# Scan stage of a two-layer block: another order of ScalarE's evictions, and the last step without its state update

## The chip, the cores and the metric

The kernel runs on one NeuronCore of a Trainium2 chip, as one program written engine by engine, with semaphores set by hand. The metric is the device time of one execution in microseconds (us). PE is TensorE, ACT ScalarE, DVE VectorE, POOL GpSimd, and SP issues the DMA transfers.

## The reference

Two layers are computed. Only the first is touched here. Its attention is a scan over mini-batches of 16 tokens (32 steps for 4 sequences of 512 tokens, 32 heads of 16), which carries a state W1, b1:

```python
def step(carry, x):
    W1_s, b1_s = carry
    xq, xk, xv, eta_mb = x
    Z1 = xk @ W1_s + b1_s
    grad = _ln_fused_l2_bwd(Z1, xv - xk, ln_w, ln_b)
    Attn1 = jnp.tril(xq @ xk.swapaxes(-1, -2))
    b1_bar = b1_s - jnp.tril(eta_mb) @ grad
    Z1_bar = xq @ W1_s - eta_mb * Attn1 @ grad + b1_bar
    W1_new = W1_s - (last_eta * xk).swapaxes(-1, -2) @ grad
    b1_new = b1_s - jnp.sum(last_eta * grad, axis=-2, keepdims=True)
    out = xq + _ln(Z1_bar, ln_w, ln_b)
    return ((W1_new, b1_new), out)
_, ys = jax.lax.scan(step, init, xs)      # the state behind the last step is dropped
```

Beside it runs the first layer's feed-forward part, which does not depend on the scan:

```python
g = jnp.einsum('th,ih->ti', xf, gate_w) * gate_s
u = jnp.einsum('th,ih->ti', xf, up_w) * up_s
hdn = jax.nn.silu(g) * u
out = jnp.einsum('ti,hi->th', hdn, down_w) * down_s
```

The second layer (latent attention and a mixture of experts) follows and makes up the larger part of the time.

## The kernel before

The stage in question is one block, from about 196 to 858 us of the span. It interleaves two kinds of work in a written order, `for n in range(END)` on every engine, END = 44. Each engine takes its own list strictly in order.

**The scan.** Steps n = 0 to 31 (`NSTEP` = 32) each carry the state once round the engines. PE computes the step's product into `zbank` (`z_product`, L833 and L836). ACT squares it (L1035), DVE reduces, ACT takes the root (L1037), and then DVE runs a chain of twelve small instructions (L1130 to L1148) that ends in the scaled gradient `sg`. DVE and ACT copy two blocks each of it into `sg_bd` (L1154, L1058). PE's `state_update` (L849) needs all four copies. DVE adds the result to `w_state` (L1088), DVE and ACT spread it into `w_x` (L1094, L949), and the next `z_product` reads that. POOL sums the gradients for the bias (`sum_s`, L721 and L723).

**The outputs of the scan** come `LAG` = 9 steps later, in groups G of four parts. `scores` (L877) needs `q_bd` from ACT (L967), DVE masks the result into `pt` (L1114), `outputs` (L903) adds to `obank`. A group is closed by ACT (`o_sb`, `o_sq`), `variances` on PE (L911), a root on ACT (`o_std`, L1043), four reciprocals on DVE (L1167), a product on POOL (L792), the scale and bias on ACT (L1024, the first thing in `late`), and an addition to `q_t` on POOL (L798). From n = 32 to 43 this work and the rest of the feed-forward part stand alone; call it the tail.

**The feed-forward part** is a list of jobs, `gate`, `up` and `down`, each a group of matmuls (L60 to L62) into one of two PSUM banks by turns, so that a job can start only when the one two places before it is evicted. The list runs gate, up, gate, up; before each third's four `down` jobs the next third's first gate has been put. A step of the scan is cut in four pieces (`ffn(n, 0)` to `ffn(n, 3)`), and a job's ACT and POOL work is done in the piece in which its last matmul falls. ACT evicts a gate with Silu (`silu_g`, L1003) and an up with a copy (L1009). POOL multiplies the two (`product`, L741). ACT rounds the product to its high half `hid_hi` (`high`, L991; in two halves at L988 near a `down`), and POOL subtracts for the low half (`low`, L747). ACT does the high half of up j-1 just ahead of the eviction of gate j.

Silu and the root are in different tables of ACT, so a load of 1.28 us (ACT_TABLE_LOAD, under L1003 or L1033) stands ahead of the first Silu behind a root.

Of the kernel before, what the change touches and what calls it, by code (L numbers as in the profile page):

```python
# [69 lines left out]
def build(nc, A, out):  # L70
    with ExitStack() as outer:
# [486 lines left out]
        with ExitStack() as st:  # L558
# [82 lines left out]
            with nc.Block() as block:  # L641
# [63 lines left out]
                def _(pool):  # L705
# [71 lines left out]
                    for n in range(END):  # L777
                        ffn(n, 0)
                        if n < NSTEP:
                            sum_s(n)  # L780
# [22 lines left out]
                def _(pe):  # L803
# [110 lines left out]
                    for n in range(END):  # L914
# [10 lines left out]
                        if n < NSTEP:  # L925
                            state_update(n)
                            if n + 1 < NSTEP:
                                turn_k(n + 1)
# [13 lines left out]
                def _(act):  # L942
# [50 lines left out]
                    def ffn(n, i):  # L993
                        for j in ended(n, i):
                            t, kind, a, o = JOBS[j]
                            x, bank = nth(j), fb[j % 2]
                            if j >= 1 and kind_of(j - 1) == "up" and kind != "down":
                                high(j - 1)
# [13 lines left out]
                            else:  # L1012
                                if x >= 2:
# [3 lines left out]
                                                     scale=small[:, SM["down_s"] + o:SM["down_s"] + o + 1]).then_inc(ev_down, 1)  # L1017

                    def late(n):
                        G = finish_at(n)  # L1020
                        if G is not None:
                            g = G % NF
                            act.wait_ge(oxh_done, G + 1)
                            nc.scalar.activation(o_y[:], o_y[:], ACT.Identity, scale=small[:, SM["ttt_w"] + g:SM["ttt_w"] + g + 1],  # L1024
                                                 bias=small[:, SM["ttt_b"] + g:SM["ttt_b"] + g + 1]).then_inc(oy_done, 1)
                        ffn(n, 3)

                    expand(0)
                    turned_k(0)
                    for n in range(END):  # L1030
# [21 lines left out]
                        if n < NSTEP:  # L1052
                            act.wait_ge(sg_done, n + 1)
                            if n == 0:
                                act.wait_ge(zero_done, 2)
                            for b in (2, 3):
                                r = slice(32 * b, 32 * b + 32)
                                nc.scalar.activation(sg_bd[r, b, :], sg[r, n % 2, :], ACT.Copy).then_inc(sgbd_act, 1)  # L1058
# [20 lines left out]
                def _(dve):  # L1079
# [44 lines left out]
                    for n in range(END):  # L1124
                        ps = parts_at(n)
                        if n < NSTEP:
# [22 lines left out]
                            dve.wait_ge(sg_done, n + 1)  # L1149
                            if n == 0:  # L1150
                                dve.wait_ge(zero_done, 2)
                            for b in (0, 1):
                                r = slice(32 * b, 32 * b + 32)
                                nc.vector.tensor_copy(sg_bd[r, b, :], sg[r, n % 2, :]).then_inc(sgbd_dve, 1)  # L1154
# [1098 lines left out]
```

## Time and profile before

| | us |
|---|---|
| median of three runs | 2019.95 (2014.51 to 2021.71) |
| the profiled execution | 2020.42 |
| its span (first to last instruction) | 2018.8 |

Busy time of the engines over the span, from the profile's page:

| engine | busy us | share |
|---|---|---|
| PE | 1879.5 | 93% |
| DVE | 1228.3 | 61% |
| POOL | 1023.7 | 51% |
| ACT | 983.4 | 49% |

PE is the busy engine in the whole program, but a mean over unlike stages says little about one of them. The stage is read by asking, for each pause of PE, which wait ended last. The releaser that a row names is the last by the profile; where a row says "issue", the profile shows none, and the instruction on the other engine that ended just before the pause has to be looked up by its time.

### The profile page before, as it was taken

To read this page: it belongs to the slowest core of one execution; us is meant where nothing else is said; L and a number is where in the kernel's file an instruction comes from. 1 tells how busy PE (TensorE), PEld (TensorE's weight loads), DVE (VectorE), ACT (ScalarE), POOL (GpSimd) and SP (SyncE) were. 2 spreads that over 40 slices of the span, in tenths; PEclk is the share of its full clock that TensorE was granted. 3 is DMA by queue.
4 is the path that set the end of the run, shared out by engine and by line. 5 is a ranking of instruction groups with operands and counts; after the bars stand their busy time and mean duration, and the time that the engine had idled before them with its cause. 6 is when DMAs were issued, how large, how long until landed. Compare 5 with 4: busy or idle time off the path is not lost. (4 is left out here: it accounts for less than half of the span.)

```text
span 2018.8 us, 34603 instructions
## 1 busy us (share of the span) xinstructions
PE 1879.5 (93%) x12536; PEld 1416.2 (70%) x12536; DVE 1228.3 (61%) x2417; ACT 983.4 (49%) x2117; POOL 1023.7 (51%) x896
## 2 busy tenths in 40 slices
PE   5898899998999999799899989999999999999998
PEld 3676777666666665487777866777777777777776
DVE  4663566688788864367345446666666666666663
ACT  3332556556565655445434335444444444444442
POOL 5444566566565644520143337555555555555552
PEclk9998999999999999989999999999999999999999
DMA  7885657336334533132678861232333223322320
GB/s 239 281 302 184 224 168 265 117 116 219 107 115 146 190 100 107 61 128 85 231 241 284 264 229 43 95 115 95 105 115 115 95 88 132 113 75 76 106 101 33
DMA packets 157111, 297.96 MB, mean 148 GB/s; under 512 B 20240, under 2 KB 97296, under 8 KB 150288
## 3 DMA queue, kind: packets, MB, share of 16 engines
q1 hardware_dynamic: 155856, 294.70, 43.3%
q8 instruction: 102, 1.67, 0.3%
q10 hardware_dynamic: 1088, 1.05, 0.2%
q14 instruction: 65, 0.53, 0.1%
HBM read 221.52 MB, written 74.19 MB: 146 GB/s over the span
## 5 line engine op out<-in xcount | busy, mean ns | idle before, releaser
L1996 POOL TENSOR_SCALAR probs<-probs,rsum 128x512 f32<-128x512 f32 x256 | 396.6, 1567 | 247.5 <-DVE rsum L2132 247.5
L2096 ACT ACTIVATE p_tok<-bank 128x512 fp32r<-128x512 f32 x256 | 154.9, 608 | 345.7 <-PE bank L2036 345.6
L2128 DVE TENSOR_REDUCE nmax<-bank 128x1 f32<-128x512 f32 x256 | 158.9, 683 | 93.7 <-PE bank L2028 93.7
L2138 DVE TENSOR_TENSOR p_tok<-bank,p_tok 128x512 fp32r<-128x512 f32 x256 | 173.4, 680 | 16.2 <-ACT p_tok L2096 16.2
L2088 ACT ACTIVATE probs<-bank,nmax 128x512 f32<-128x512 f32 x256 | 173.0, 693 | 2.2 <-DVE nmax L2128 2.2
L60 PE MATMUL bank<-xs,ffn_w 128*128 128x512 f32 x352 | 154.9, 440 | 12.7 <-issue 9.2
L1484 POOL TENSOR_TENSOR y_pieces<-y_tok,y_pieces 128x512 fp32r<-128x512 f32 x48 | 64.2, 1351 | 188.4 <-ACT y_pieces L1689 188.4
L2036 PE MATMUL bank<-ident,probs 128*128 128x128 f32 x1024 | 156.5, 277 | 2.8 <-DVE p_tok L2138 2.8
L2036 PEld LDWEIGHTS bank<-ident,probs 128*128 128x128 f32 x1024 | 122.4, 141 | 51.0 <-issue 27.4
L61 PE MATMUL bank<-xs,ffn_w 128*128 128x512 f32 x352 | 140.4, 399 | 0.0
L62 PE MATMUL bank<-xs,ffn_w 128*128 128x512 f32 x352 | 140.1, 398 | 0.0
L1114 DVE SCALAR_TENSOR_TENSOR pt<-bank,t_mask 128x256 f32<-128x256 f32 x256 | 91.8, 414 | 77.5 <-PE bank L877 76.0
L741 POOL TENSOR_TENSOR hid<-up_down_sb,silu_g 128x256 f32<-128x256 f32 x88 | 66.6, 777 | 101.7 <-issue 76.7
L759 POOL TENSOR_TENSOR ff_acc<-ff_acc,up_down_sb 128x256 f32<-128x256 f32 x96 | 73.5, 790 | 81.0 <-ACT up_down_sb L1016 81.0
L60 PE MATMUL bank<-p_tok,ckv_tok 128*128 128x512 f32 x256 | 106.2, 415 | 5.5 <-DVE qk L1303 2.9
L2024 PE MATMUL bank<-qk 64*128 64x512 f32 x768 | 106.9, 410 | 3.1 <-PEq L1381 3.1
L2144 DVE TENSOR_TENSOR ctx<-bank,ctx 128x512 fp32r<-128x512 f32 x64 | 44.3, 692 | 102.1 <-ACT ctx L2104 102.1
L60 PEld LDWEIGHTS bank<-xs,ffn_w 128*128 128x128 f32 x352 | 67.6, 192 | 50.8 <-issue 35.4
L60 PE MATMUL bank<-ctx,uvo 128*128 128x512 f32 x240 | 99.9, 416 | 2.3 <-issue 2.3
L62 PE MATMUL bank<-p_tok,ckv_tok 128*128 128x512 f32 x256 | 100.6, 393 | 0.0
L61 PE MATMUL bank<-p_tok,ckv_tok 128*128 128x512 f32 x256 | 100.1, 391 | 0.0
L62 PE MATMUL bank<-ctx,uvo 128*128 128x512 f32 x240 | 94.9, 395 | 0.0
(281 smaller groups left out, 4930.8 us busy)
## 6 DMA issues: line engine op xcount, KB each, us to landing
ffn_w<-ffn_pieces SPq DMA_DIRECT2D x120, 512.0 KB, 3.7
uvo<-uvo_pieces SPq DMA_DIRECT2D x15, 2048.0 KB, 7.8
wq<-wq_pieces SPq DMA_DIRECT2D x16, 1536.0 KB, 6.4
ffn_pieces<-stage SPq DMA_DIRECT2D x30, 512.0 KB, 4.2
xs<-xn_pieces SPq DMA_DIRECT2D x4, 2048.0 KB, 8.0
y_tok<-in_gup SPq DMA_DIRECT2D x32, 256.0 KB, 3.7
wk<-wk_pieces SPq DMA_DIRECT2D x16, 512.0 KB, 3.7
ffn_w<-ffn_pieces SPq DMA_DIRECT2D x16, 384.0 KB, 3.5
```

The costliest lines, as they stand in the source:

```text
L60: nc.tensor.matmul(o, w_hi, x_hi, start=start, stop=False)
L61: nc.tensor.matmul(o, w_hi, x_lo, start=False, stop=False)
L62: return nc.tensor.matmul(o, w_lo, x_hi, start=False, stop=stop)
L759: ins = nc.gpsimd.tensor_tensor(acc[:, o, h], acc[:, o, h], dn_sb[:, d % 2, h], ALU.add)
L1114: nc.vector.scalar_tensor_tensor(out=pt[:, p % 2, i, :, :], in0=psp[i][:, 0:2 * SUPER].rearrange("p (h t) -> p h t", h=2), scalar=1.0, in1 ...
L1996: nc.gpsimd.tensor_scalar(probs[:, u % 8, :], probs[:, u % 8, :], rsum[:, u % 8:u % 8 + 1], None, ALU.mult).then_inc(norm_done, 1)
L2024: nc.tensor.matmul(banks[hh][:], ten[r, a, 0, tile, q], ten[r, b, 1, tile, :], start=(a + b == 0), stop=False)
L2036: ins = nc.tensor.transpose(banks[4 + u % 2][:, kt * P:(kt + 1) * P], probs[:, u % 8, kt * P:(kt + 1) * P], ident[:])
L2088: nc.scalar.activation(probs[:, u % 8, :], banks[u % HG][:], ACT.Exp, bias=nmax[:, u % 8:u % 8 + 1], scale=1.0, accum_out=rsum[:, u % 8:u ...
L2096: nc.scalar.activation(p_tok[:, Q % 2, 0, :, hh * P:(hh + 1) * P], banks[4 + u % 2][:].rearrange("p (k q) -> p k q", k=NBLK), ACT.Copy).th ...
L2128: nc.vector.tensor_reduce(nmax[:, u % 8:u % 8 + 1], banks[u % HG][:], axis=X_AXIS, op=ALU.max, negate=True).then_inc(max_done, 1)
L2138: nc.vector.tensor_tensor(p_tok[:, Q % 2, 1, :, q], banks[4 + u % 2][:].rearrange("p (k q) -> p k q", k=NBLK), p_tok[:, Q % 2, 0, :, q].bi ...
```

## The change

Three things are changed, all in the scan stage.

1. In ACT's `ffn`, where a gate follows an up and is not itself followed by a `down`, the gate is evicted first and the up's high half is taken behind it. This holds for 32 gates. A gate right ahead of a `down` keeps the old order.
2. The scale of a group's outputs (L1024 before) is taken out of the head of `late`: for n < 32 it now stands behind `ffn(n, 3)`, for n >= 32 still ahead of it.
3. At the last step of the scan PE's `state_update`, the four copies into `sg_bd` and POOL's `sum_s` are left out.

```diff
@@ gpsimd
-                        if n < NSTEP:
+                        if n + 1 < NSTEP:
                             sum_s(n)
@@ tensor
-                        if n < NSTEP:
+                        if n + 1 < NSTEP:
                             state_update(n)
-                            if n + 1 < NSTEP:
-                                turn_k(n + 1)
+                            turn_k(n + 1)
@@ scalar
-                            if j >= 1 and kind_of(j - 1) == "up" and kind != "down":
+                            after_up = j >= 1 and kind_of(j - 1) == "up" and kind != "down"
+                            if after_up and kind_of(j + 1) == "down":
                                 high(j - 1)
                             act.wait_ge(f_ready, j + 1)
...
+                            if after_up and kind_of(j + 1) != "down":
+                                high(j - 1)
+
+                    def scale_output(n):
...
+                    def late(n):
+                        if n >= NSTEP:
+                            scale_output(n)
                         ffn(n, 3)
+                        if n < NSTEP:
+                            scale_output(n)
...
-                        if n < NSTEP:
+                        if n + 1 < NSTEP:
                             act.wait_ge(sg_done, n + 1)
@@ vector
-                            dve.wait_ge(sg_done, n + 1)
...
-                                nc.vector.tensor_copy(sg_bd[r, b, :], sg[r, n % 2, :]).then_inc(sgbd_dve, 1)
+                            if n + 1 < NSTEP:
+                                dve.wait_ge(sg_done, n + 1)
...
+                                    nc.vector.tensor_copy(sg_bd[r, b, :], sg[r, n % 2, :]).then_inc(sgbd_dve, 1)
```

ACT's list at the start of step 15 before, from the root of the step (`st_s`) to its copies of the gradient (`o_std` is a group's outputs, `hid_hi` the high half, `silu_g` an evicted gate, `up_down_sb` an evicted up):

```order
L1037 ACTIVATE st_s<-st_v,eps 128x16
L1024 ACTIVATE o_std<-o_std,small 128x512
L991 ACTIVATE hid_hi<-hid 128x512
L1003 ACT_TABLE_LOAD
L1003 ACTIVATE silu_g<-bank,ffn_scales 128x512
L967 ACTIVATE q_bd<-q_t,cols 128x128 x2
L1009 ACTIVATE up_down_sb<-bank,ffn_scales 128x512
L991 ACTIVATE hid_hi<-hid 128x512
L1003 ACTIVATE silu_g<-bank,ffn_scales 128x512
L967 ACTIVATE q_bd<-q_t,cols 128x128 x2
L977 ACTIVATE grad_bd<-grad_j 128x4x16 x2
L1058 ACTIVATE sg_bd<-sg 32x256 x2
```

The same place in the changed kernel:

```order
L1045 ACTIVATE st_s<-st_v,eps 128x16
L1003 ACT_TABLE_LOAD
L1003 ACTIVATE silu_g<-bank,ffn_scales 128x512
L990 ACTIVATE hid_hi<-hid 128x512
L1026 ACTIVATE o_std<-o_std,small 128x512
L966 ACTIVATE q_bd<-q_t,cols 128x128 x2
L1009 ACTIVATE up_down_sb<-bank,ffn_scales 128x512
L1003 ACTIVATE silu_g<-bank,ffn_scales 128x512
L990 ACTIVATE hid_hi<-hid 128x512
L966 ACTIVATE q_bd<-q_t,cols 128x128 x2
L976 ACTIVATE grad_bd<-grad_j 128x4x16 x2
L1066 ACTIVATE sg_bd<-sg 32x256 x2
```

The table load and the gate's eviction have come forward past the scale of the outputs and the high half; the number of table loads in the whole list is the same, 62. The scale of outputs passes a feed-forward eviction in five steps (14, 18, 22, 26 and 30); in 14 and 18 that eviction is a gate's with a table load.

PE's list at the last step of the scan, with the rows that are gone marked:

```order
 L61 MATMUL bank7<-xs,ffn_w 128x512
 L62 MATMUL bank7<-xs,ffn_w 128x512
-L849 MATMUL bank0<-sg_bd,ktz 32x64 x16
 L903 MATMUL bank1<-pt,grad_bd 32x128 x8
 L60 MATMUL bank7<-xs,ffn_w 128x512
```

Behind the feed-forward matmuls PE now goes straight to a group's outputs, which need nothing of this step's gradient.

## Rows read from the trace of the kernel before

**Rows 1.** Windows: the 32 scan steps; us, busy time (x instructions), clock, DMA share, GB/s.

```profile
196.00:741.00 545.00, 501.37 (x4758) 356.53 (x4759) 406.06 (x838) 324.90 (x686) 328.19 (x389) 0.98 0.50 165
```

**Rows 2.** Waits of PE, 196 to 742 us: total us, times, longest us.

```profile
PE bank L60 <- issue: 14.5, 12, 2.1
PE bank L849 <- DVE sg_bd L1154: 13.9, 15, 1.9
```

**Rows 3.** Timeline of ACT, step 15: start us, us, instruction, [idle before <-releaser].

```profile
453.90 0.80 ACT L1024 ACTIVATE o_std<-o_std,small 128x512 f32<-128x512 f32 x1
454.60 0.62 ACT L991 ACTIVATE hid_hi<-hid 128x512 fp32r<-128x512 f32 x1
455.24 1.28 ACT L1003 ACT_TABLE_LOAD   x1
456.53 0.69 ACT L1003 ACTIVATE silu_g<-bank,ffn_scales 128x512 f32<-128x512 f32 x1
...
463.52 0.85 ACT L1058 ACTIVATE sg_bd<-sg 32x256 f32<-32x256 f32 x2
```

**Rows 4.** Timeline of PE, step 15: next gate's first matmul, state update.

```profile
457.32 0.58 PE L60 MATMUL bank<-xs,ffn_w 128*128 128x512 f32 x1 [2.05 <-issue]
...
464.47 0.65 PE L849 MATMUL bank<-sg_bd,ktz 128*32 128x64 f32 x32 [0.35 <-issue]
```

**Rows 5.** Timeline of ACT and of PE, step 4.

```profile
272.54 0.63 ACT L991 ACTIVATE hid_hi<-hid 128x512 fp32r<-128x512 f32 x1 [1.87 <-POOL hid L741]
...
275.27 0.47 PE L60 MATMUL bank<-xs,ffn_w 128*128 128x512 f32 x1 [0.76 <-issue]
...
279.55 0.65 PE L849 MATMUL bank<-sg_bd,ktz 128*32 128x64 f32 x32
```

**Rows 6.** Timeline of DVE, ACT and PE, step 12: copies of the gradient, state update.

```profile
409.92 0.77 DVE L1154 COPY sg_bd<-sg 32x256 f32<-32x256 f32 x2
410.55 0.85 ACT L1058 ACTIVATE sg_bd<-sg 32x256 f32<-32x256 f32 x2
411.50 0.65 PE L849 MATMUL bank<-sg_bd,ktz 128*32 128x64 f32 x32 [1.27 <-DVE sg_bd L1154]
```

**Rows 7.** Timeline of ACT and PE, step 25.

```profile
638.67 0.85 ACT L1058 ACTIVATE sg_bd<-sg 32x256 f32<-32x256 f32 x2 [1.46 <-DVE sg L1148]
...
639.65 0.65 PE L849 MATMUL bank<-sg_bd,ktz 128*32 128x64 f32 x32
```

**Rows 8.** Timeline of ACT and PE, step 31 and the first matmul of step 32.

```profile
744.71 0.85 ACT L1058 ACTIVATE sg_bd<-sg 32x256 f32<-32x256 f32 x2
745.66 1.08 PE L849 MATMUL bank<-sg_bd,ktz 128*32 128x64 f32 x32 [3.88 <-issue]
...
754.18 1.13 PE L911 MATMUL bank<-o_sq,avg 128*128 128x512 f32 x2
```

**Rows 9.** Line L1144 (DVE, two SBUF inputs): ns least/median/most, first and last start us.

```profile
L1144 DVE TENSOR_TENSOR t<-t x32: 424/638/930, 209.0 to 741.1; 128x256 f32<-128x256 f32 x32
```

**Rows 10.** Timeline of POOL, ACT and PE, steps 32 and 33.

```profile
758.09 1.43 POOL L747 TENSOR_TENSOR hid_lo<-hid,hid_hi 128x256 fp32r<-128x256 f32 x2 [4.13 <-ACT hid_hi L991]
759.47 1.29 POOL L730 TENSOR_TENSOR w_snap_x<-w_snap,bd 128x512 f32<-128x512 f32 x1
762.24 1.29 POOL L792 TENSOR_TENSOR o_std<-o_sb,o_std 128x512 f32<-128x512 f32 x1 [1.48 <-DVE o_std L1167]
763.56 0.81 ACT L1024 ACTIVATE o_std<-o_std,small 128x512 f32<-128x512 f32 x1 [3.26 <-POOL o_std L792]
765.01 0.71 PE L877 MATMUL bank<-q_bd,k_t 32*128 32x256 f32 x8 [0.88 <-ACT q_bd L967]
```

**Rows 11.** Windows behind and in long pauses of PE: columns as in rows 1.

```profile
457.60:460.90 3.30, 3.30 (x9) 2.52 (x8) 3.06 (x8) 1.41 (x3) 1.62 (x2) 0.50 0.18 66
...
600.30:602.20 1.90, 0.00 (x0) 0.00 (x0) 1.76 (x5) 1.89 (x3) 0.81 (x2) 1.00 0.25 101
602.30:605.70 3.40, 3.40 (x41) 2.14 (x45) 2.34 (x6) 1.81 (x7) 1.75 (x2) 1.00 0.24 73
```

More of the change, by code:

```diff
@@ L1017, in ffn @@
                                                      scale=small[:, SM["down_s"] + o:SM["down_s"] + o + 1]).then_inc(ev_down, 1)
-                    def late(n):
+                            if after_up and kind_of(j + 1) != "down":
+                                high(j - 1)
+                    def scale_output(n):
                         G = finish_at(n)
@@ L1148, in _ @@
                             nc.vector.tensor_tensor(hd(sg[:, n % 2, :]), hd(t1[:]), over_d(st_f[:]), ALU.mult).then_inc(sg_done, 1)
-                            dve.wait_ge(sg_done, n + 1)
[L1150 to L1153, printed above, removed]
-                                nc.vector.tensor_copy(sg_bd[r, b, :], sg[r, n % 2, :]).then_inc(sgbd_dve, 1)
+                            if n + 1 < NSTEP:
+                                dve.wait_ge(sg_done, n + 1)
+                                if n == 0:
+                                    dve.wait_ge(zero_done, 2)
+                                for b in (0, 1):
+                                    r = slice(32 * b, 32 * b + 32)
+                                    nc.vector.tensor_copy(sg_bd[r, b, :], sg[r, n % 2, :]).then_inc(sgbd_dve, 1)
                         if ps:
```

## The prediction

> **What bounds the kernel now.** I read the windows first. In the 545 us of the 32 scan steps PE is busy for 501, at a mean clock of 0.98 [rows 1]: 44 us are pauses, and only they can be won by another order. Next PE's waits, to see what the pauses are. Two kinds lead: 14.5 us in 12 pauses ahead of a feed-forward job (L60, "issue"), and 13.9 us in 15 pauses ahead of the state update, L849 [rows 2]. Last the timelines of PE and ACT side by side, step by step, because a pause of the first kind is worth only what the second kind leaves of it: if PE comes earlier to L849 but `sg_bd` isn't ready, it waits there instead.
>
> **The pause behind a gate.** Step 15 shows the mechanism. PE pauses 2.05 us until 457.32 [rows 4]; ACT in that time scales the outputs (from 453.90), takes a high half, loads the Silu table (1.28) and ends the gate's eviction at 456.53 + 0.69 = 457.22 [rows 3]. PE had finished the gate long before. In the new order the table load comes first, at 453.99, so the eviction ends at 453.99 + 1.29 + 0.69 = 455.97, or 1.25 earlier. The scale (0.80, less 0.1 of overlap) and the high half (0.62) run behind it, beside PE.
>
> Then comes the part that is easily missed. L849 started at 464.47, just behind ACT's copies, which ended at 463.52 + 0.85 = 464.37 [rows 3, 4]. So ACT's list decides this step. It was late because the next gate ran at half clock (below) and its eviction stood ahead of the copies. Counted again from 455.97 (high half 456.6, scale 457.4, `q_bd` 457.9, up 458.5, then POOL's product until 460.1, high half 460.8, `q_bd` and `grad_bd` 461.8, copies 462.7) L849 starts at 462.8. That is 1.65 us gained, not 2.05. Step 19 is the twin (pause 2.01); there the same count gives 1.1. Together 2.75 us.
>
> **Shorter pauses.** Steps 4, 6, 8 and 22 have pauses of 0.5 to 0.9 us before a gate's second successor. In step 4 the pause is 0.76, ACT waited 1.87 for POOL's product with the table load and the eviction queued behind [rows 5], and L849 had no pause of its own. The new order evicts during that wait: 0.7 gained. For 6 and 8 I take 0.6 each, for 22 only 0.25, since `sg_bd` is nearly as late there. Sum 2.15 us. In step 23 the up's eviction passes the scale of the outputs and the chain behind it ends 0.6 earlier, with room at L849: 0.6.
>
> **ACT's copies later than DVE's.** In step 12 DVE ends its copies at 409.92 + 0.77 = 410.69, ACT at 410.55 + 0.85 = 411.40, and L849 follows at 411.50 [rows 6]. The profile names DVE; it was ACT. ACT was held by high half, table load and eviction in a row, and the first of these waited for POOL. With load and eviction done during that wait ACT is in time. Four steps are of this kind (12, 18, 21, 28): between 0.45 and 0.9 each, 2.6 us.
>
> **No gain, or a loss.** In step 25 the pause ahead of the gate can go, but L849 at 639.65 stands 0.13 behind ACT's copies (638.67 + 0.85 = 639.52) [rows 7]: nothing is won, and step 29 is its twin. More than that: a later high half puts POOL's subtraction later into DVE's chain. DVE's addition L1144 takes 424 ns at the least and 930 at the most [rows 9], 424 where POOL stands still. A two-instruction overlap more costs 0.4. I count it for steps 3, 25 and 29, and 0.2 for step 11, against 0.8 gained in step 1, where a subtraction leaves the chain altogether. Net -0.6 us. The bounds are -4 and +4 us for the whole stage, half an instruction's difference (0.25) in 16 steps either way.
>
> The Trainium skill says of this ("SBUF — State Buffer", Who interferes with whom) that a VectorE instruction with two SBUF inputs and a GpSimd instruction that reads SBUF exclude each other, and that the one that comes second is blocked whole, whichever it is. By that rule the loss in steps 3, 25 and 29 can as well fall on POOL, which has time there; the -0.6 would be +0.6 and the sum below 13.8. The median of L1144, 638 ns, lies halfway between its ends, so DVE is the one that loses often enough here, and I stay with the rows.
>
> **The last step.** ACT's copies end at 744.71 + 0.85 = 745.56, L849 pauses 3.88 and starts at 745.66, and step 32 starts at 754.18 [rows 8]. Without L849 PE goes on at 741.78. What it then needs (mask and gradient of the part before) is ready. Up to step 32 lie outputs 0.65, half a job 1.65, base 1.6, scores 0.7, three matmuls 0.9, outputs 0.65, at full clock. That makes 747.8, thus 6.4 us earlier: 3.88 of pause, 1.08 less an overlap for L849 itself, and the rest because the stretch from 745.7 ran at half clock, which follows from the long pause. What comes next late would be ACT's `o_sb`, needed by base at 744.1, and ACT is free at 743. The copies on DVE and ACT and the two sums on POOL were beside it and bring nothing more. Bounds: 4.5 (the half clock comes all the same) to 6.6.
>
> **The tail.** Here a high half ahead of a gate stands on the path. In step 32 POOL subtracts from 758.09, spreads the snapshot, is done at 760.76, and takes the product L792 at 762.24, which ACT's scale and then PE's scores wait for [rows 10]. The subtraction moves from 758.09 to about 760.15 (ACT loads the table and evicts first, 1.28 + 0.69), POOL ends at 762.9, 0.65 too late. Once more in step 33, where the addition to `q_t` is behind it. Cost 1.3 us; bounds 0 and 2.
>
> **Sum.** 2.75 + 2.15 + 0.6 + 2.6 - 0.6 + 6.4 - 1.3 = 12.6 us. I take 1.6 off for the clock. Behind the 2.05 us pause PE ran 3.3 us at 0.50 [rows 11], that is 1.2 GHz; behind the pause in step 23 it kept 1.00, 2.4 GHz [rows 11]. Before, half clock in steps 15 and 19 fell in a piece that waited anyway. Now the pause (some 2 us in step 19) sits right ahead of L849, and half clock behind it is on the path, 1.65 us each time. The Trainium skill says ("TensorE: Matmul & The Clock Gate", What's actually happening) that the clock is set by how busy PE has lately been; which pause is punished it can't tell us here, nor can the rows. So 11.0 us: from the profiled 2020.42 that is 2009.4, from the median, which is 0.47 below it, 2009.0. The stage ends at a barrier, so nothing behind it gives any of this back.
>
> **Rivals.**
> 1. *The scan gives it all back at L849.* 13.9 us of waits there [rows 2] show how near the bound is. Then the last step less the tail remains, 6.4 - 1.3 = 5.1: 2014.9. Against it: steps 4, 12 and 15, read above, have room.
> 2. *The clock falls twice on the path*, in steps 15 and 19: 12.6 - 3.3 = 9.3, so 2010.7.
> 3. *More is won*: no half clock in the scan at all, also not behind step 11's pause of 1.9 us at L849, 1.6 us, and DVE's chain meets POOL less (2 us): 2003.8.
> 4. *POOL becomes the bound, and it is slower.* POOL works in order, and 32 subtractions are 0.65 us or more later. In the tail this is 0.65 a time. If the scan paid it each time, it would be 30 x 0.65 = 19.5 plus the tail's 1.3, less 6.4: +14.4, 2034.4. It decides from some 17 payments on. Against it: PE's waits name no product of POOL among the first, and in the steps read the subtraction is followed by a wait.
> 5. *It doesn't do what it says*: the table load stays behind the gate's last matmul, or PE's pause at the last step turns into one for `o_sb`. Some 0 to 2 us, about 2019.
>
> **How the numbers follow.** Forecast 0.46, rival 1 0.20, 2 0.14, 3 0.12, 4 0.05, 5 0.03. 0.5%, about what a measurement can tell from no change, is 10.1 us: faster means under 2009.85. The forecast's own range is 2006 to 2012.5, about 0.6 of it faster. With a third of rival 2 and all of rival 3: faster 0.45, same 0.50, slower 0.05. The range, 2003.5 to 2015.5, reaches over rivals 1 to 3.
>
> **What would show it.** In the trace after: ACT's table load right behind `st_s` in step 15 and PE's pause there at about 0.8; L849 in step 15 still right behind ACT's copies; step 31 without a pause ahead of L903; from the last step's z to `variances` of step 32 about 14 us instead of 20.6; a pause of 1.5 instead of 0.88 ahead of the scores of step 33. PE's waits ahead of L60 for "issue" fall from 14.5 to about 7, those ahead of L849 stay or grow by some 2 us. The forecast is wrong if the scan steps 1 to 30 together don't shorten by 4 us or more, or if half clock stands behind an L849.

## The result, and the profile after

| | before | after |
|---|---|---|
| median, 5 runs each | 2019.06 us (2014.51 to 2021.71) | 2006.89 us (2006.27 to 2008.36) |
| ratio to before | | 0.9944, 95% interval 0.9929 to 0.9959 |
| profiled execution (span) | 2020.42 (2018.8) | 2006.43 (2004.8) |

The changed kernel is 0.56% faster. 2009.0 was forecast, within 2003.5 to 2015.5. Line numbers of the scan stage are up to 9 higher after: ACT's copies of the gradient L1066, DVE's L1163, DVE's chain L1138 to L1156, POOL's lines the same.

The scan in both kernels, by the first product of step 1 and of step 31. Timeline of PE, before, then after: start us, us, instruction.

```profile
220.22 0.38 PE L833 MATMUL bank<-s_sum,bd 128*128 128x256 f32 x1
...
732.26 0.48 PE L833 MATMUL bank<-s_sum,bd 128*128 128x256 f32 x1
```

```profile
219.66 0.38 PE L833 MATMUL bank<-s_sum,bd 128*128 128x256 f32 x1
...
727.50 0.48 PE L833 MATMUL bank<-s_sum,bd 128*128 128x256 f32 x1
```

512.04 us have become 507.84, 4.2 less. PE's waits over the scan, after (total us, times, longest us), which answer to [rows 2]:

```profile
PE bank L849 <- DVE sg_bd L1163: 18.8, 21, 2.4
PE bank L60 <- issue: 7.9, 10, 1.7
```

Pauses ahead of feed-forward jobs are halved (14.5 to 7.9), and three quarters of it stand now ahead of the state update (13.9 to 18.8). The windows after show the clock behind two pauses, in steps 7 and 11; columns as in [rows 1].

```profile
317.30:320.70 3.40, 3.40 (x9) 2.63 (x9) 3.30 (x4) 0.23 (x1) 3.08 (x4) 0.50 0.64 192
392.40:395.80 3.40, 3.40 (x24) 2.27 (x23) 1.61 (x5) 2.97 (x7) 1.71 (x2) 0.50 0.13 42
```

Step 15, timelines of ACT and of PE after, beside [rows 3, 4]:

```profile
452.84 1.28 ACT L1003 ACT_TABLE_LOAD   x1
454.13 0.69 ACT L1003 ACTIVATE silu_g<-bank,ffn_scales 128x512 f32<-128x512 f32 x1
454.72 0.62 ACT L990 ACTIVATE hid_hi<-hid 128x512 fp32r<-128x512 f32 x1
455.24 0.80 ACT L1026 ACTIVATE o_std<-o_std,small 128x512 f32<-128x512 f32 x1
...
460.58 0.85 ACT L1066 ACTIVATE sg_bd<-sg 32x256 f32<-32x256 f32 x2
```

```profile
454.92 0.47 PE L60 MATMUL bank<-xs,ffn_w 128*128 128x512 f32 x1 [0.79 <-issue]
...
461.53 0.65 PE L849 MATMUL bank<-sg_bd,ktz 128*32 128x64 f32 x32 [1.40 <-DVE sg_bd L1163]
```

The pause fell from 2.05 to 0.79, as counted. L849 still stands 0.1 behind ACT's copies (460.58 + 0.85 = 461.43) and now pauses 1.40 itself, so most of what the first pause lost stands at the second. The step is 1.78 us shorter all the same, and windows of the whole steps 15 and 19, before and then after, say why:

```profile
451.04:471.74 20.70, 18.04 (x172) 12.52 (x168) 14.72 (x32) 12.79 (x29) 11.76 (x14) 0.92 0.39 117
522.92:543.30 20.38, 18.04 (x172) 12.59 (x168) 15.30 (x33) 12.68 (x27) 11.19 (x12) 0.92 0.30 91
```

```profile
449.88:468.80 18.92, 16.52 (x172) 11.39 (x168) 15.36 (x32) 12.79 (x29) 11.31 (x14) 1.00 0.41 123
519.80:538.69 18.89, 16.36 (x172) 11.39 (x168) 14.86 (x33) 12.56 (x27) 10.71 (x12) 1.00 0.33 98
```

PE's idle time (length less PE busy) went from 2.66 to 2.40 us in step 15 and from 2.34 to 2.53 in step 19. Of the 3.27 us that the two steps are shorter, 3.2 are therefore PE's own work, which no longer meets half clock. Over the whole scan PE's idle time fell by 1.9 us (512.04 - 474.25 against 507.84 - 471.96), and its busy time by 2.3: half clock came three times before (steps 11, 15, 19) and twice after (7 and 11).

In the last step `outputs` starts at 736.62 without a pause, beside the 745.66 of L849 in [rows 8], and step 32 at 742.23:

```profile
736.62 0.65 PE L903 MATMUL bank<-pt,grad_bd 128*32 128x128 f32 x16
...
742.23 1.13 PE L911 MATMUL bank<-o_sq,avg 128*128 128x512 f32 x2
```

From z of step 31 to there it is 14.7 us instead of 21.9 (the prediction's 14 and 20.6 count from the end of the product, 1.3 us later). The tail, timelines of POOL and of PE after, beside [rows 10]:

```profile
748.48 1.42 POOL L747 TENSOR_TENSOR hid_lo<-hid,hid_hi 128x256 fp32r<-128x256 f32 x2 [6.11 <-ACT hid_hi L990]
749.86 1.28 POOL L730 TENSOR_TENSOR w_snap_x<-w_snap,bd 128x512 f32<-128x512 f32 x1
751.10 1.30 POOL L792 TENSOR_TENSOR o_std<-o_sb,o_std 128x512 f32<-128x512 f32 x1
```

```profile
753.88 0.71 PE L877 MATMUL bank<-q_bd,k_t 32*128 32x256 f32 x8 [1.33 <-ACT q_bd L966]
```

POOL waits 6.11 instead of 4.13, and its product L792 follows the snapshot at once, where it had 1.48 of room. The pause ahead of the scores is 1.33 instead of 0.88.

**Where 14.0 us of the profiled execution went.** The stage starts 0.8 earlier (198.88 instead of 199.70), its step 0 is 0.3 longer, the scan 4.2 shorter, the last step 7.2 shorter, the tail (from variances of step 32 to the next stage's first matmul) 105.41 instead of 104.35, 1.1 longer. That makes 10.9. The other 3.1 lie behind the stage, in code that nobody changed. Over the fourteen profiles of this study that remainder takes from 1152.5 to 1161.8 us, with no order in it. So 10.3 us lie in the stretches that the change touches (11.7 in a second profile of the changed kernel, see below), and 3.7 in code that it doesn't; nothing ties these to the change.

### The profile page after: what moved, and what is told of

The parts are those of the page before. It is cut to its first block and busy times, and to the rows that moved or that the text cites. A ratio compares the mean times of both kernels' runs of the same rounds, so it can differ in the third digit from the quotient of the medians.

```text
span 2004.8 us, 34531 instructions
## 1 busy us (share of the span) xinstructions
PE 1875.6 (94%) x12504; PEld 1414.9 (71%) x12504; DVE 1224.2 (61%) x2415; ACT 979.8 (49%) x2115; POOL 1022.7 (51%) x894
## 5 line engine op out<-in xcount | busy, mean ns | idle before, releaser
L60 PE MATMUL bank<-xs,ffn_w 128*128 128x512 f32 x352 | 152.9, 434 | 6.7 <-issue 3.4
L61 PE MATMUL bank<-xs,ffn_w 128*128 128x512 f32 x352 | 138.8, 394 | 0.0
L62 PE MATMUL bank<-xs,ffn_w 128*128 128x512 f32 x352 | 138.6, 394 | 0.0
L1122 DVE SCALAR_TENSOR_TENSOR pt<-bank,t_mask 128x256 f32<-128x256 f32 x256 | 91.6, 413 | 72.7 <-PE bank L877 71.3
L60 PE MATMUL bank<-p_tok,ckv_tok 128*128 128x512 f32 x256 | 106.2, 415 | 5.4 <-DVE qk L1312 2.9
L747 POOL TENSOR_TENSOR hid_lo<-hid,hid_hi 128x256 fp32r<-128x256 f32 x88 | 66.4, 775 | 83.2 <-ACT hid_hi L990 77.7
L60 PE MATMUL bank<-ctx,uvo 128*128 128x512 f32 x240 | 99.8, 416 | 2.2 <-issue 2.2
L60 PEld LDWEIGHTS bank<-xs,ffn_w 128*128 128x128 f32 x352 | 66.6, 189 | 43.0 <-issue 27.6
```

What stands on the lines that cost most here:

```text
L60: nc.tensor.matmul(o, w_hi, x_hi, start=start, stop=False)
L61: nc.tensor.matmul(o, w_hi, x_lo, start=False, stop=False)
L62: return nc.tensor.matmul(o, w_lo, x_hi, start=False, stop=stop)
L1122: nc.vector.scalar_tensor_tensor(out=pt[:, p % 2, i, :, :], in0=psp[i][:, 0:2 * SUPER].rearrange("p (h t) -> p h t", h=2), scalar=1.0, in1 ...
```

## The experiments

Because the stage is read from one profile, the useful measure is the length of a step (first L833 of a step to that of the next). It repeats: apart from step 0 and steps with half clock, two kernels with the same order in a step agree in nearly all steps within 0.05 us. The exceptions are step 16, which took 0.27 more at full clock in two of the fourteen profiles, and step 24, 0.2 more in two; why is open. Medians are weaker, since the remainder moves by some us. The lengths in this table are from the profiles. The last column is the device time, to be set against the kernel before in the same rounds: 2018.15 for the parts alone and the old order in the tail, 2018.03 (one run) from "old scale in step 26" to "small subtraction", 2014.59 (one run) for "subtraction behind" and "both", 2018.48 for "all together" and "changed, again".

| kernel | scan, steps 1 to 30 | last step | tail | device median |
|---|---|---|---|---|
| before | 512.04 | 21.92 | 104.35 | 2019.06 |
| changed | 507.84 | 14.72 | 105.41 | 2006.89 |
| changed, again | 506.53 | 14.71 | 105.40 | 2009.37 |
| last step alone | 511.96 | 16.66 | 104.83 | 2015.61 |
| gates alone | 509.22 | 17.47 | 105.71 | 2011.66 |
| scale alone | 511.34 | 19.75 | 104.74 | 2014.10 |
| old order in the tail | 508.10 | 14.71 | 104.42 | 2008.09 |
| old scale in step 26 | 507.40 | 14.72 | 105.49 | 2005.21, one run |
| gate 28 old | 508.44 | 14.72 | 105.43 | 2013.20, one run |
| picked order | 504.07 | 14.72 | 104.40 | 2000.16, one run |
| small subtraction | 495.50 | 14.72 | 103.28 | 1994.30, one run |
| subtraction behind | 507.22 | 14.71 | 104.35 | 2004.91, one run |
| both | 503.04 | 14.72 | 104.39 | 1998.44, one run |
| all together | 504.25 | 14.71 | 104.43 | 2001.52 |

### The three parts, each alone

```diff
 # last step alone: before, with (the copies and POOL's sums likewise)
-                        if n < NSTEP:
+                        if n + 1 < NSTEP:
                             state_update(n)
 # gates alone: before, with
-                            if j >= 1 and kind_of(j - 1) == "up" and kind != "down":
+                            after_up = j >= 1 and kind_of(j - 1) == "up" and kind != "down"
+                            if after_up and kind_of(j + 1) == "down":
                                 high(j - 1)
...
+                            if after_up and kind_of(j + 1) != "down":
+                                high(j - 1)
 # scale alone: before, with
+                        if n >= NSTEP:
+                            scale_output(n)
                         ffn(n, 3)
+                        if n < NSTEP:
+                            scale_output(n)
```

> The kernel before with the last step alone changed (no state update, copies into sg_bd or sums for it; the state behind that step is read by nobody). Theory: the pause of 3.88 us ahead of L849, L849 itself and the half clock behind it go, and nothing else moves: from the last step's first z to variances of step 32 it takes 14.7 us as in the changed kernel instead of 21.9, so the median falls by 6.4 to 7.2, to about 2012. Steps 1 to 30 stay within 0.3 us of before in sum, unless the clock drops elsewhere. Rival (the ACT order was what won the last step): the stretch stays above 20 us and the gain is under 2 us. Rival (half of the gain was clock that comes back elsewhere): the stretch takes 17 to 18 us.

> The kernel before with only the gates' evictions put ahead of the high half (32 gates, tail too). Theory: the scan's short pauses go (step 1 -0.9, 4 -0.6, 8 -0.5, 12 -0.7, 28 -0.7); in steps 15 and 19 the scale of the outputs still stands ahead of the table load, so they gain some 0.7 less each than the 1.8 and 1.5 of the changed kernel, that is about 1.1 and 0.8; the pause of 2.0 in step 23 stays; step 27 stays at 17.6 instead of 18.3, because there only the later scale lets POOL's addition start 6 us earlier and meet DVE's chain. From z of step 1 to z of step 31 -2.5 to -4 us, tail +1.4: the median falls by 1 to 3 us, to about 2017. Rival (part 1 alone makes all the gain of steps 15 and 19): these two shorten by 3.3 us together. Rival (the loss in step 27 comes from the later high half): step 27 takes 18.3 us here too.

> The kernel before with only the scale of a group's outputs put behind ffn(n, 3) for n < 32. Theory: steps 15, 19 and 23 each win the 0.7 to 0.8 us of the scale (step 23 the 1.0 of the changed kernel), step 27 loses 0.7 because POOL's addition of a down comes into DVE's chain (z to sg 9.1 instead of 8.0 us), all others stay: -1.5 to -2.5 us in the scan, median about 2017. Rival (the two parts have nothing to do with each other and step 27's loss is the high half's): step 27 stays at 17.6 and the sum is -2.5 to -3.2. Rival (the scale alone brings nothing, since the copies of the gradient decide steps 15 and 19): these two stay within 0.2 us.

Against before the ratios are 0.9982 (0.9971 to 0.9993), 0.9966 (0.9952 to 0.9980) and 0.9983 (0.9971 to 0.9996). All three are faster, but the medians missed what was expected: 2015.61 instead of about 2012, 2011.66 and 2014.10 instead of about 2017.

*Last step alone.* It won 5.3 of the 7.2 us, outside of what theory and rivals gave. Timelines of PE and ACT, last step:

```profile
744.40 0.45 PE L888 MATMUL bank<-of_seq,s_snap_hi 128*128 128x512 f32 x1 [1.32 <-ACT o_sb L1067]
```

```profile
740.27 0.63 ACT L990 ACTIVATE hid_hi<-hid 128x512 fp32r<-128x512 f32 x1 [2.03 <-POOL hid L741]
740.92 1.28 ACT L1002 ACT_TABLE_LOAD   x1
...
743.68 0.58 ACT L1067 ACTIVATE o_sb<-bank 128x512 f32<-128x512 f32 x1
```

The pause that the prediction named as next in line, `o_sb`, comes when the gate isn't evicted during the wait for POOL's product. So the last step's gain needs the gate's order as well; the steps 1 to 30 stayed within 0.1 us in sum.

*Gates alone.* Steps 15 and 19 won 1.4 and 1.1, more than the 1.1 and 0.8 expected. Step 27 stayed at 17.64: its loss isn't the gates'. The last step won 4.5 without any work left out, because L849 paused 1.89 instead of 3.88 and no half clock came. *Scale alone.* Step 23 won 0.75 and step 27 lost 0.69, as expected. Steps 15 and 19 won 1.1 and 1.3, more than the 0.7 to 0.8 of the scale, and by the clock: PE's idle time in them rose, to 3.17 and 2.67 us, while neither had half clock any more. Step 16 took 1.8 more, 0.3 of it a longer pause ahead of L849 and the rest behind half clock from 484.4 to 487.8. The parts don't add up: in the last step alone they give 5.3 + 4.5 + 2.2 = 11.9 against 7.2 together, since each takes away a share of the same pause (3.88 us, then 3.00 with the scale alone, 1.89 with the gates alone) and all or half of the same half clock.

In steps 15 and 19 half clock goes with the length of the pause ahead of the gate's second successor: it stood behind the pauses of 2.0 us in both kernels with the old order there (before, last step alone), and in none of the other twelve profiles, where these pauses are 0.7 to 1.5 us. So in these two steps the shorter pause and the clock at 2.4 GHz came together each time; how long the old order would take there at full clock, no run shows. It is no rule either: step 7, below, pauses 1.96 in every kernel and has half clock in six of the fourteen.

### The tail, and step 27

```diff
 # old order in the tail
-                            if after_up and kind_of(j + 1) == "down":
+                            late_high = after_up and kind_of(j + 1) != "down" and n < NSTEP
+                            if after_up and not late_high:
                                 high(j - 1)
...
-                            if after_up and kind_of(j + 1) != "down":
+                            if late_high:
                                 high(j - 1)
 # old scale in step 26
-                        if n >= NSTEP:
+                        if n >= NSTEP or n == 26:
                             scale_output(n)
```

> The changed kernel with the old order (high half, then gate) for the gates of steps 32 to 43. Theory: POOL's subtractions in the tail come 2 us earlier again, the pauses ahead of the scores of steps 33 and 34 are 0.88 and 0.69 instead of 1.33 and 1.24, and from variances of step 32 to the end of the stage it takes 1.4 us less, as before: median 2005.5. The scan's steps stay the same. Rival (the tail's 1.4 us came from something else, such as the clock or when the transfers land): the tail stays at 98.1 us and the median at 2006.9.

> The changed kernel with the scale of outputs ahead of ffn(26, 3) again, one step of thirty-two. Theory: in the changed kernel the eviction of a down job no longer waits for the scale, so POOL's addition (L759) starts 3.9 us earlier against DVE, at the reciprocal's end, and DVE's small instructions, 424 ns each, take up to 900 beside it: z to sg 9.08 us in step 27. With the old order there z to sg is 8.03 again and step 27 takes 17.63 us instead of 18.31, all other steps the same. Rival (the loss comes from a high half put behind its gate): step 27 stays at 18.3. Rival (the pause of 2.17 us ahead of L849 is made by ACT's copies): z to sg falls but the step doesn't.

The tail fell by 1.0, not 1.4, and the pause of step 33 is back at 0.87. The median, 2008.09, can't show so little. Step 27 fell from 18.31 to 17.61, all others stayed. The cause shows in the timelines of POOL and DVE in step 27. The changed kernel first:

```profile
662.62 1.62 POOL L759 TENSOR_TENSOR ff_acc<-ff_acc,up_down_sb 128x256 f32<-128x256 f32 x2 [1.22 <-ACT up_down_sb L1016]
```

```profile
662.00 0.25 DVE L1138 RECIPROCAL st_r<-st_s 128x16 f32<-128x16 f32 x1 [0.38 <-ACT st_s L1045]
...
662.75 0.90 DVE L1140 TENSOR_TENSOR gx_gt_xh<-gx_gt_xh,w_tile 128x256 f32<-128x256 f32 x1
663.68 0.84 DVE L1142 TENSOR_TENSOR gx_gt_xh<-gx_gt_xh,cst 128x256 f32<-128x256 f32 x1
...
666.88 1.00 DVE L1149 SCALAR_TENSOR_TENSOR t<-st,gx_gt_xh 128x256 f32<-128x256 f32 x1
667.92 0.59 DVE L1151 TENSOR_TENSOR st_f<-st_r,lr 128x16 f32<-128x16 f32 x1
...
669.00 0.43 DVE L1156 TENSOR_TENSOR sg<-t,st_f 128x256 f32<-128x256 f32 x1
```

and with the old scale in step 26:

```profile
662.85 1.78 POOL L759 TENSOR_TENSOR ff_acc<-ff_acc,up_down_sb 128x256 f32<-128x256 f32 x2 [1.92 <-ACT up_down_sb L1016]
```

```profile
661.53 0.25 DVE L1138 RECIPROCAL st_r<-st_s 128x16 f32<-128x16 f32 x1 [0.38 <-ACT st_s L1045]
...
662.27 0.42 DVE L1140 TENSOR_TENSOR gx_gt_xh<-gx_gt_xh,w_tile 128x256 f32<-128x256 f32 x1
662.73 0.42 DVE L1142 TENSOR_TENSOR gx_gt_xh<-gx_gt_xh,cst 128x256 f32<-128x256 f32 x1
663.19 0.84 DVE L1143 TENSOR_TENSOR gx_gt_xh<-gx_gt_xh 128x256 f32<-128x256 f32 x1
...
667.06 0.84 DVE L1156 TENSOR_TENSOR sg<-t,st_f 128x256 f32<-128x256 f32 x1
```

POOL's addition of a down job starts 0.62 us behind L1138 instead of 1.32, that is 0.70 earlier against the chain, not the 3.9 that the expectation said; that figure was wrong. It doubles L1140 and L1142 in place of L1143. The chain is then 0.5 later, POOL's product comes 0.4 earlier, and they meet at L1149 and L1151, with the old scale only at L1156. From L1138 to the end of `sg` it takes 669.43 - 662.00 = 7.43 instead of 667.90 - 661.53 = 6.37. The Trainium skill ("SBUF — State Buffer", Who interferes with whom) has the two engines share a pair of ports as an exclusive lock, and these rows agree in that a DVE instruction with two inputs doubles while POOL works. L1144, a reduction with one input, took 0.95 in both kernels, though POOL's addition lay partly beside it only with the old scale.

### Gate 28, the clock, and the picked order

```diff
 # gate 28 old (late_high used as in the edit of the tail)
+                            late_high = after_up and kind_of(j + 1) != "down" and j != 28
 # picked order, with the old scale in step 26 beside it
+                            late_high = after_up and kind_of(j + 1) != "down" and n < NSTEP and j not in (14, 28, 48, 84, 94, 108)
```

> The changed kernel with the old order for one gate alone, the 29th job, whose eviction falls in the first piece of step 6. Theory: with it the pause ahead of the down job in step 6 is 0.45 us again instead of 0.97, and without two pauses so near together the clock doesn't fall behind the pause of 1.96 us in step 7: step 6 stays at 16.65 us (what the earlier gate won was lost at that pause), step 7 takes 16.69 instead of 18.29, and the stage ends 1.6 us earlier. Rival (half clock in step 7 has to do with where in time the pause falls, not with what went before): step 7 stays at 18.3 or the half clock comes in another place. Rival (POOL lateness made step 7 long): the step stays at 18.3 with the clock at full speed.

> The changed kernel with the old order at six gates (the jobs 14, 28, 48, 84, 94 and 108, in steps 3, 6, 11, 22, 25 and 29), in the tail, and for the scale in step 26: everywhere that the changed kernel lost time. Theory: each is on its own, so the scan wins 0.2 + 1.6 + 0.35 + 0.15 + 0.6 + 0.7 + 0.65 = 4.2 us more than the changed kernel (z of step 1 to z of step 31 503.6 instead of 507.8) and the tail half a microsecond to 1.4; device time about 2002. Rival (the clock hits back: half clock comes behind another pause once it isn't spent in step 7): 1.6 to 3.3 us less of it. Rival (what one step wins the next gives back): z to z stays above 506.

> The changed kernel itself once more, for a comparison in the same rounds. Theory (the order of the work in the stage repeats, and with it where the clock falls): each scan step within 0.05 us of the first profile, half clock again in steps 7 and 11, median 2006 to 2009. Rival (half clock falls at random): it comes behind other pauses, and steps differ by 1.6 us.

The theory on gate 28 fell. Step 6 didn't change at all: the pause ahead of job 28 waits for the eviction of job 26, two places before, so the wrong gate was put back. Step 7 had half clock all the same (320.6 to 324.0). What did move is elsewhere: none in step 11, one in step 27. It could be put down to the edit only until the changed kernel ran again and showed just these two, and no half clock in step 7 either. So its expectation (half clock again in steps 7 and 11) fell, and the rival holds; at full clock all other steps came within 0.05 us of the first profile except step 24, 0.2 longer. Its windows behind the same pauses of steps 7 and 11 as above, and in step 27:

```profile
315.30:318.70 3.40, 3.36 (x15) 2.82 (x16) 3.26 (x5) 1.17 (x2) 3.40 (x5) 1.00 0.67 216
388.00:391.40 3.40, 3.30 (x59) 2.40 (x59) 2.56 (x7) 2.17 (x5) 2.68 (x4) 1.00 0.27 77
666.70:670.10 3.40, 3.40 (x23) 2.38 (x24) 1.86 (x5) 2.72 (x6) 1.96 (x3) 0.51 0.94 365
```

The first two pauses ahead of them are those of the first profile, 1.96 and 2.40. Timeline of PE, changed kernel again:

```profile
315.34 0.47 PE L60 MATMUL bank<-hid_hi,ffn_w 128*128 128x512 f32 x1 [1.97 <-ACT up_down_sb L1016]
...
387.99 0.61 PE L849 MATMUL bank<-sg_bd,ktz 128*32 128x64 f32 x29 [2.42 <-DVE sg_bd L1163]
...
665.89 0.65 PE L849 MATMUL bank<-sg_bd,ktz 128*32 128x64 f32 x32 [2.07 <-DVE sg_bd L1163]
```

So 1.2 or 2.4 GHz behind one and the same pause of 2 us changes from execution to execution. The price can be read where both were seen: step 7 18.29 or 16.69, step 11 20.00 or 18.56, step 27 19.66 or 18.31: 1.35 to 1.6 us. The Trainium skill ("TensorE: Matmul & The Clock Gate", What's actually happening) ties the clock to PE's recent activity; these rows don't contradict it, and don't show what singles out one pause.

The picked order took 504.07 us for the scan, as expected (503.6), though for other reasons in part: steps 3, 22, 25, 27 and 29 won 0.17, 0.20, 0.47, 0.70 and 0.64, step 11 won 0.4 beside its half clock of 1.4, step 7 kept its own, step 23 lost 0.25. The expected sum counted 1.6 for step 7 that didn't come. The tail is back at 104.40.

### POOL's subtraction against DVE's chain

```diff
 # small subtraction (from the fifth on)
+                            if q >= 4:
+                                h = slice(h.start, h.start + 8)
                             ins = nc.gpsimd.tensor_tensor(hid_lo[:, slot, h], hid[:, q % 2, h], ...
 # subtraction behind, with the old order in the tail and the old scale in step 26
 # ("both": the six gates old as well)
+                            pool.wait_ge(hlo_done, q - 1)
...
-                                low(nth(j - 1))
+                                later.append(nth(j - 1))
+                                if i > 0 or not 1 <= n < NSTEP - 1 or kind_of(j + 1) == "down":
+                                    flush()
...
                             sum_s(n)
+                        flush()
                         ffn(n, 1)
```

> The changed kernel with POOL's subtraction for the low half done on 8 columns of each half instead of 256 from the fifth on (part of the feed-forward result is left out); every wait and signal stays. Theory: what makes DVE's chain long is POOL's work beside it, so z to sg falls in the steps where a subtraction lies in the chain (3, 11, 16, 19, 22, 25, 29: by 0.4 to 1.0 us each) and stays in those where none does (2, 12, 13, 28, at 7.4 to 7.5); as these steps have a pause ahead of L849, they shorten by as much: the scan by 3 to 8 us. In the tail the half microsecond of the later subtraction goes too, twice. Rival (DVE's times don't hang on POOL's subtraction but on its product and sums): z to sg stays within 0.2 us in all steps and the scan within 1 us. Rival (POOL in order is the bound): also steps without a pause ahead of L849 shorten, the scan by over 15 us.

> The changed kernel with POOL's subtraction for the low half, where it falls in the first piece of a step and no down job follows at once, put behind the sums of the step's gradient, that is behind DVE's chain; and with the old order in the tail and for the scale in step 26. All gates of the scan keep the new order. Theory (POOL beside DVE's chain is what costs): z to sg falls to about what the run with the small subtraction showed (steps 3, 6, 11, 16, 21, 22, 25, 29: 0.4 to 1.0 us less than in the changed kernel), and since nothing else is late, z of step 1 to z of step 31 is 500 to 503 us instead of 507.8, less than the 504.1 of the picked order. Rival (the subtraction costs the same wherever it lies, because DVE adds and spreads the state behind the gradient and POOL's bias factors come later): the scan stays at 505 to 508. Rival (a down job waits for its low half): pauses of over 0.5 us ahead of the down jobs in steps 5, 13, 16, 26.

> As the run before, with the old order too at the gates 14, 28, 48, 84, 94 and 108. Theory: with the subtraction out of the chain a gate's early eviction costs nothing any more, so the old order at these six can only lose: 0 to 1.5 us more than the run before in the scan. Rival (the loss at these gates had another cause than POOL's subtraction, such as ACT's list): this run is 1.5 to 2.5 us faster than the run before, as the picked order was against the changed kernel.

The small subtraction leaves out part of the result, and so shows a cost, not a kernel to use. With it the scan is 12.3 us shorter, of which some 3 are two half clocks that didn't come; the other 9 are more than the theory's 8. Steps 3, 21, 22, 25, 26 and 29 won 0.6 to 0.9, step 6 1.3 (a down job waits for the subtraction there). Steps 12 and 28, where nothing was expected, won 0.36, though z to sg stayed at 7.5 us there. The timelines of DVE in step 12 say where it lies, the changed kernel first, then the small subtraction:

```profile
408.58 1.45 DVE L1163 COPY sg_bd<-sg 32x256 f32<-32x256 f32 x2
```

```profile
403.91 0.81 DVE L1165 COPY sg_bd<-sg 32x256 f32<-32x256 f32 x2
```

There POOL's subtraction (from 408.21, 1.68 us) lies beside the two copies of the gradient, right behind the chain, and stretches those instead. L849 comes only 0.09 earlier for it; the rest is won at DVE's mask L1122 behind the copies, for which PE waits 0.22 in the changed kernel (ahead of L861) and not with the small subtraction. Step 28 shows the same 1.45 and 0.82.

Where the subtraction is put behind the gradient it helps as well. Step 25 in the changed kernel, POOL and DVE:

```profile
629.90 1.61 POOL L747 TENSOR_TENSOR hid_lo<-hid,hid_hi 128x256 fp32r<-128x256 f32 x2 [4.59 <-ACT hid_hi L990]
631.47 1.60 POOL L741 TENSOR_TENSOR hid<-up_down_sb,silu_g 128x256 f32<-128x256 f32 x2
```

```profile
630.04 0.89 DVE L1149 SCALAR_TENSOR_TENSOR t<-st,gx_gt_xh 128x256 f32<-128x256 f32 x1
630.96 0.58 DVE L1151 TENSOR_TENSOR st_f<-st_r,lr 128x16 f32<-128x16 f32 x1
631.58 0.90 DVE L1152 TENSOR_TENSOR t<-t 128x256 f32<-128x256 f32 x1
632.52 0.85 DVE L1156 TENSOR_TENSOR sg<-t,st_f 128x256 f32<-128x256 f32 x1
```

Four of DVE's instructions in a row are doubled or more beside two of POOL's in a row. Before, the copies there stood 0.13 ahead of L849 [rows 7]; now PE waits 1.07. With the subtraction behind the gradient step 25 takes 16.90 us (before 17.23, changed 17.83). Step 3 takes 14.69, 21 16.20, 22 15.69. Against that stand down jobs that now wait for their low half, POOL's row "hid_lo" among PE's waits of the kernel "subtraction behind":

```profile
PE bank L60 <- POOL hid_lo L748: 4.4, 3, 1.9
```

in steps 4, 6 and 26 (the 1.4 us in step 26 stand in the changed kernel as well), and half clock in steps 6, 11, 13 and 23, by the same steps of "both" an estimated 5.7 us in sum. The scan as a whole, 507.22, missed the expected 500 to 503; only step by step does it speak for the theory. In "both", which had none, steps 3, 22, 25 and 29 took 14.84, 16.30, 17.35 and 17.70 where "subtraction behind" took 14.69, 15.69, 16.90 and 17.45. So once the subtraction is out of the chain the early gate is the better order in all four, and the rival falls: what made the change lose there was POOL's place, not ACT's. The sum hides it, since "both" is 4.2 us shorter: less the 5.7 of half clock it is 1.5 longer, the upper end of what was expected.

### All together

The old order in the tail, for gate 108 and for the scale in step 26, and the subtraction behind the gradient in eight steps (3, 11, 12, 18, 21, 22, 25, 28).

> What the runs point to, together: the changed kernel with the old order in the tail, at gate 108 and for the scale in step 26, and POOL's subtraction put behind the gradient in steps 3, 11, 12, 18, 21, 22, 25 and 28 alone, where no down job waits for it. Theory: each step takes the least time that it had in any of the runs; against the picked order that is 0.5 + 0.35 + 0.3 + 0.4 + 0.9 + 0.5 + 0.45 + 0.3 = 3.7 us less in the scan, 500.4 us from z of step 1 to z of step 31 if half clock comes once as there, 498.8 if never; median about 1997. Rival (the clock decides): half clock comes behind two to four pauses, each 1.6 us, and the scan is at 502 to 505. Rival (the steps are not independent): other steps than these lengthen at full clock by over 0.3 us.

2001.52 us (1998.29 to 2005.98), ratio to before 0.9919 (0.9903 to 0.9935); the changed kernel, timed beside it, 2009.37 (2007.38 to 2014.78), 0.9958 (0.9941 to 0.9975). It is faster than both, but slower than the 1997 expected. The clock took its share. Windows behind three pauses:

```profile
391.20:394.60 3.40, 3.40 (x19) 2.44 (x12) 1.60 (x4) 2.48 (x6) 2.57 (x3) 0.51 0.02 5
421.90:425.30 3.40, 3.40 (x15) 1.82 (x14) 1.56 (x6) 1.27 (x4) 0.51 (x1) 0.50 0.23 20
596.00:599.40 3.40, 3.40 (x34) 2.37 (x38) 1.91 (x5) 1.44 (x3) 1.74 (x2) 0.51 0.26 77
```

Steps 11, 13 and 23 are 1.2 to 1.6 longer than in the picked order, the scan is at 504.25 instead of 500.4 or less, as the rival on the clock had it (502 to 505). The other rival came true too, that steps aren't independent: step 29 took 17.74 at full clock, against 17.26 in the picked order. With the subtraction of step 28 behind the gradient it lies beside DVE's copy into `w_x` (1.34 us instead of 1.00). DVE's reciprocals for the outputs start 2.31 us ahead of step 29 instead of 2.82, the root and ACT's list behind it come 0.47 later, and the pause ahead of the gate's second successor is 1.32 instead of 0.86. Steps 12 and 13 are such a pair as well: the pause in step 13 is 2.08 instead of 1.61. So in steps 12 and 28 the move won 0.3 and cost the next step 0.5.

## Why the prediction was right, and where it was not

The size came out because errors cancelled. Step by step, in us, from the two profiles:

| step of the prediction | predicted | measured |
|---|---|---|
| steps 15 and 19 | -2.75 | -3.27 |
| short pauses, steps 4, 6, 8, 22 | -2.15 | -0.99 |
| step 23 | -0.6 | -1.04 |
| copies of ACT late, steps 12, 18, 21, 28 | -2.6 | -2.01 |
| POOL against DVE, steps 1, 3, 11, 25, 29 | +0.6 | +0.88 |
| step 27 | 0 | +0.68 |
| half clock | +1.6, in 15 or 19 | +1.6, in step 7 |
| last step | -6.4 | -7.20 |
| tail | +1.3 | +1.06 |
| sum | -11.0 | -10.3 |

- **The pause behind a gate** was right in the order of events: table load first, 0.79 left, L849 behind ACT's copies. The terms were 0.13 too small in step 15 (1.65, measured 1.78) and 0.39 in step 19 (1.1, measured 1.49). What the prediction had wrong is its sentence that half clock in these steps "fell in a piece that waited anyway". The windows above show PE's idle time nearly unchanged and its busy time 3.2 us shorter, so that half clock was paid in full there, and its absence is nearly all that PE gained.
- **Shorter pauses** is the step that failed, by half. Steps 4 and 8 gave 0.61 and 0.53, but step 6 nothing: the pause ahead of job 28 fell from 0.92 to 0.40 and the one ahead of a down job in the same step grew from 0.45 to 0.97. Step 22 lost 0.16: DVE's chain, met by the subtraction, took more than the pause gave back.
- **ACT's copies later than DVE's** held; step 18 gave 0.16 of 0.45, as L849 then waited for DVE.
- **POOL against DVE** was named and priced (0.4 for an overlap more), and steps 25 and 29 lost 0.60 and 0.65, since subtraction and product follow each other in the chain; step 3 lost only 0.18, step 11 0.34 for 0.2. Not foreseen was that part 2 does the same: with the scale behind it, a down job's eviction frees POOL's addition earlier, and step 27 lost 0.68. The prediction counted the scale's move as free.
- **The last step** went as written, and it needs the gates' order to do so: alone it wins 5.3. Its size was 0.8 low. The list of what lies up to step 32 adds up to 6.15 us, which gives 747.9 and a gain of 6.25, not 6.4, PE needed 5.61 from `outputs` to step 32 (742.23 - 736.62), and `outputs` started 9.12 us behind z instead of the 9.52 counted.
- **The clock**: an amount was taken off, and it fell due in a step that the change doesn't touch. That was luck: with the same kernel it was 1.35 in step 27 another time, and none in steps 7 and 11. The forecast named half clock behind an L849 as a sign against it. There was one in step 11, where before had it too, and in the second profile one in step 27, where before had none; by that sign the forecast failed on the clock. Its other sign, 4 us less in the scan, was met by 0.2.
- **Rivals.** The first (all given back at L849) took 4.9 of the 6.6 us that L60's pauses lost, where the prediction expected some 2. The scan still won 4.2, but only 1.9 of it in idle time of PE, so of the pauses themselves this rival had the greater part right. POOL was no bound in order: in the tail its lateness cost 1.1, in the scan it cost through DVE.

How much the two kernels differ beyond that can't be told finely: 12.2 us between the medians of the first runs, 9.1 in the later ones, around the 10.3 and 11.7 of the stage's two profiles.

## What to carry to other kernels

When instructions are moved on one engine, look at what each releases on the others, and where that lands: in step 27 an eviction 0.7 us earlier let POOL's addition into DVE's chain and cost 0.68 us. Split the length of a step into idle and busy time before calling it a shorter wait: in steps 15 and 19 the pauses mostly changed places, and the gain stood in busy time, at full clock. Work out the last step of a loop for what nobody reads; it was the largest gain in one place here, 5.3 us by itself. And where remainder and clock move by some us from run to run, compare lengths of steps inside profiles, and run one kernel twice before a half clock is put down to an edit.

## What was not expected of the hardware

- Behind one and the same pause of 1.96 us PE ran at 1.2 GHz in one execution and at 2.4 GHz in the next, and likewise behind 2.4 us; where a step was seen both ways, half clock cost 1.35 to 1.6 us.
- In step 27 DVE's chain takes 6.37 us beside one addition and one product of POOL, and 7.43 when they land otherwise, with the same instructions on both engines; a small one of 128x16 went from 0.17 to 0.59 us.
- Outside the clock nearly every step of the stage repeats to 0.05 us, while unchanged code behind the stage varied by 9 us over fourteen profiles.
